# Sixteen small loads of each chunk's update, issued behind the seventh group's gradient loads

## The reference

```
step: g  = gradient of mean((mlp(params, k_t) - v_t)**2) by the parameters
      m  = eta_t * m - theta_t * g
      p  = (1 - alpha_t) * p + m
      out_t = mlp(p, q_t)           # after the new parameters
mlp(z) = silu(z @ (W0 + P0)) @ (W1 + P1)
```

## Time and profile before

| | |
|---|---|
| median of three runs | 12295.05 us |
| the profiled execution | 12288.19 us |
| its span | 12286.5 us |
| mean granted clock of TensorE | 0.881 of full |
| TensorE matmuls busy | 9695.2 us, 79 % |
| VectorE busy | 4669.4 us, 38 % |
| ScalarE busy | 1960.7 us, 16 % |
| GpSimd busy | 232.7 us, 2 % |
| DMA | 519.70 MB, mean 42 GB/s |

### The profile page before, as it was taken

One profiled execution on the slowest core, in us unless ns is written; L12 is line 12 of the kernel. 1 busy time (PEld: TensorE's weight loads), 2 busy tenths in 40 slices (PEclk: granted clock), 3 DMA queues, 4 the chain that ended last, 5 costly groups with the idle time before them and its releaser, 6 DMA issues. The chain is left out here.

```text
span 12286.5 us, 338221 instructions
## 1 busy us (share of the span) xinstructions
PE 9695.2 (79%) x135922; PEld 5708.6 (46%) x135922; DVE 4669.4 (38%) x11974; ACT 1960.7 (16%) x4398; POOL 232.7 (2%) x167
## 2 busy tenths in 40 slices
PE   5788883523598888888988988889888898896777
PEld 2455551212355555555555555555455555552222
DVE  3444443634723323233233233232332323235555
ACT  1222221211101101011011011110101101012334
POOL 0000000000100000000000000000000000000000
PEclk7999996555898998999999999989898798987888
DMA  2000000143601101011011011120211202020000
GB/s 55 7 7 8 7 8 25 42 123 61 138 17 53 51 18 52 23 47 53 17 53 53 17 53 57 42 81 17 82 45 54 81 17 82 26 72 14 13 10 10
DMA packets 894399, 519.70 MB, mean 42 GB/s; under 512 B 379950, under 2 KB 889462, under 8 KB 892534
## 3 DMA queue, kind: packets, MB, share of 16 engines
q1 hardware_dynamic: 880694, 502.37, 15.1%
q0 software_dynamic: 13312, 12.57, 0.6%
HBM read 323.24 MB, written 154.20 MB: 39 GB/s over the span
## 5 line engine op out<-in xcount | busy, mean ns | idle before, releaser
L2319 PE MATMUL bank<-mv,hdiag 128*32 128x144 f32 x63744 | 2038.0, 289 | 102.1 <-DVE hdiag L2480 102.1
L2319 PEld LDWEIGHTS bank<-mv,hdiag 128*32 128x32 f32 x63744 | 1950.0, 111 | 165.8 <-DVE hdiag L2480 151.2
L2359 PE MATMUL bank<-mvt,ydiag 128*32 128x512 f32 x15936 | 1830.3, 594 | 0.0
L2359 PEld LDWEIGHTS bank<-mvt,ydiag 128*32 128x32 f32 x15936 | 606.5, 109 | 807.8 <-issue 723.1
L2493 DVE TENSOR_TENSOR rep<-bank,wt 128x128 f32<-128x128 f32 x249 | 92.0, 369 | 1863.1 <-PE bank L2319 1863.1
L439 PE MATMUL att_bank<-att_ka,att_qn 128*124 128x496 f32 x1024 | 497.0, 598 | 133.6 <-DVE att_mx L616 67.0
L2423 DVE SCALAR_TENSOR_TENSOR mvt<-mvt,cu,bank 128x256 f32<-128x256 f32 x512 | 223.3, 478 | 791.3 <-PE bank L2254 791.3
L2216 ACT ACTIVATE work<-work 128x128 f32<-128x128 f32 x498 | 142.3, 309 | 2357.6 <-DVE work L2468 2357.6
L2203 ACT ACTIVATE mv<-bank 128x256 f32<-128x256 f32 x1024 | 325.1, 384 | 1091.1 <-PE bank L2267 1091.1
L459 PE MATMUL att_bank<-att_qa,att_ka 128*124 128x248 f32 x2048 | 464.7, 385 | 32.6 <-DVE att_qa L625 32.6
L2254 PE MATMUL bank<-hist,wy 32*128 32x256 f32 x2048 | 393.1, 544 | 90.4 <-DVE wy L2413 89.7
(11 more groups left out here) (402 smaller groups left out, 11450.9 us busy)
## 6 DMA issues: line engine op xcount, KB each, us to landing
hdiag<-between_slopes SPq DMA_DIRECT2D x368, 512.0 KB, 4.6
baset<-between_base SPq DMA_DIRECT2D x265, 128.0 KB, 2.0
between_base<-work SPq DMA_DIRECT2D x256, 128.0 KB
hist<-h SPq DMA_DIRECT2D x1992, 8.0 KB
hist<-y SPq DMA_DIRECT2D x1992, 2.0 KB
hist<-dl SPq DMA_DIRECT2D x1992, 8.0 KB
ct<-between_table SPq DMA_DIRECT2D x184, 128.0 KB, 3.8
between_slopes<-key_zero SPq DMA_DIRECT2D x8, 2048.0 KB
```

The source lines that it names most:

```text
L2319: mm = e.matmul(psP[32 * j:32 * j + 32, 0:MW], hdiag[:, hf, r, j, :], mv1[:, hf, r, j, :], start=(hf == 0 and r == 0), stop=(hf == 1 and r ...
L2359: mm = e.matmul(psH[32 * j:32 * j + 32, :], ydiag[:, n, j, :], mvt[:, 4 * n + j, :], start=(n == 0), stop=(n == 7))
```

## The change

The two loops that issue the sixteen loads become a function, `rows_of_table`. It is called in the loop over g, at g = 6, behind that group's gradient loads. The number of loads, their sources, targets and semaphores are as before.

```diff
+        def rows_of_table(e, c):
+            for i in range(8):
+
+                src = CT[bass.ds(c, 1), bass.ds(64 + c * CH, CH), :, :].rearrange("a s (m i) f -> s (a m) i f", m=2)[:, :, i, :]
+                e.dma_start(ccp[16 * i:16 * i + 16, 0:16 * CH].rearrange("p (m f) -> p m f", m=2), src).then_inc(cc_in.sem, 16)
+            for q in range(8):
+                row = CT[bass.ds(c, 1), bass.ds(64 + c * CH, 1), 0:1, :].rearrange("a s g f -> (a s g) f")
+                src = bass.AP(row.tensor, row.offset + (16 * q + 1), [[128, 16], [2049, CH - 1], [1, 1]])
+                e.dma_start(alt[16 * q:16 * q + 16, 1:CH].unsqueeze(2), src, allow_slow_non_contiguous=True).then_inc(al_in.sem, 16)
...
                     for xk in range(DX):
                         load_slopes(e, part, xk)
-                    for i in range(8):
...
-                        e.dma_start(ccp[16 * i:16 * i + 16, 0:16 * CH].rearrange("p (m f) -> p m f", m=2), src).then_inc(cc_in.sem, 16)
-                    at = 0
-                    for q in range(8):
...
-                        e.dma_start(alt[16 * q:16 * q + 16, 1:CH].unsqueeze(2), src, allow_slow_non_contiguous=True).then_inc(al_in.sem, 16)
                     for g in range(16):
                         e.wait_ge(T.sem, T.upd(c, f"bg{g}"))
                         settled(e, s_own)
...
                         if g % 2 and g // 2 + 2 < 8:
                             load_table(e, c, part, g // 2 + 2)
+                        if g == 6:
+                            rows_of_table(e, c)
                         if g % 2:
                             e.wait_ge(A.sem, A.upd(c, f"bs{g // 2}"))
```

More of the change, by code:

```diff
@@ L2133, in chunk @@
                         load_slopes(e, part, xk)
-                    for i in range(8):
-                        src = CT[bass.ds(c, 1), bass.ds(64 + c * CH, CH), :, :].rearrange("a s (m i) f -> s (a m) i f", m=2)[:, :, i, :]
-                        e.dma_start(ccp[16 * i:16 * i + 16, 0:16 * CH].rearrange("p (m f) -> p m f", m=2), src).then_inc(cc_in.sem, 16)
-                    at = 0
-                    for q in range(8):
-                        row = CT[bass.ds(c, 1), bass.ds(64 + c * CH, 1), 0:1, :].rearrange("a s g f -> (a s g) f")
-                        src = bass.AP(row.tensor, row.offset + (16 * q + 1), [[128, 16], [2049, CH - 1], [1, 1]])
-                        e.dma_start(alt[16 * q:16 * q + 16, 1:CH].unsqueeze(2), src, allow_slow_non_contiguous=True).then_inc(al_in.sem, 16)
                     for g in range(16):
```

## The result

The changed kernel takes 12356.81 us (median of four runs, 12350.34 to 12372.16), the kernel before 12291.96 us (four runs, 12281.11 to 12295.21). The ratio is 1.0056 with a 95 % interval of 1.0039 to 1.0074: it is slower by 0.56 %; the medians lie 65 us apart. The forecast was slower, 12397 us, in a range of 12335 to 12440. The direction and the range held; the size was too large by 40 us. The profiled execution's span is 12348.7 us, 62.2 us over the one before.

A forecast was written before the change was run, and what follows sets the result against it. TensorE sets the pace in the update, its waits for gradient loads being all the change can remove. Idle 32.2, clock 64.4 and 4.6, late chunks 1.1: 102.3 us slower, 12397 us on the runs' scale, range 12335 to 12440 us.

The forecast's parts named there:

- Nothing is gained in the early chunks' front: Chunks 0 to 8, front of the update: no load wait behind the sixteen, so moving them away saves 0.
- The late chunks' front wait goes: Chunks 9 to 15, group 1's second product: waits of 4.9 us in six, 3.02 in chunk 15 go; 32.4 us saved.
- Group 10's table rows come late: Chunks 0 to 8, group 10: TensorE idles 4.3 us in seven, 2.1 in chunk 1, none in chunk 3; 32.2 us.
- The middle wait of the late chunks: Chunks 9 to 15, group 8's second product: idle of 4.7 us in six, 5.3 in chunk 9; 33.5 us added.
- The clock falls with the idle: Chunks 0 to 8, behind group 10's 4.3 us idle: granted clock falls from 1.00 to near 0.5 to 0.7.
- What the fall costs: Chunks 0 to 8, group 10 to L2112: half-clock time adds 64.4 us in seven chunks, 4.6 in chunk 1.
- The rival in which the clock returns after 5 us: Behind the middle idle, full clock returns at once or after 5 us: +48, 12343 us; chance 0.13.
- The step put at nothing: Chunks 0 to 8, update up to group 7: moving the sixteen from the front saves 0, no clock change counted.
- The faster rival: Chunks 9 to 15: group 8's idle brings full clock back, -73 us; sum -40, 12255 us; chance 0.05.

The follow-up runs named there:

- Experiment 7: Changed kernel with the burst cut in two: eight cc loads behind group 6's gradient loads, eight alt behind group 10's; 12263.66 us, 0.9985 of the kernel before.
- experiment 2: Kernel before, with the sixteen loads moved behind group 6's gradient loads in chunks 9 to 15 alone; 12285.37 us, 1.0010 of the kernel before.
- Experiment 3: Changed kernel plus seven idle matmuls ahead of group 10's table-row wait in chunks 0 to 8; 12305.99 us, 1.0023 of the kernel before.
- experiment 8: One cc and one alt load behind each even group's gradient loads, idle matmuls in group 0's waits and late chunks' second-load waits; 12204.51 us, 0.9935 of kernel before.
- experiment 6: One cc and one alt load behind each even group's gradient loads, idle matmuls in group 0's two waits; 12239.70 us, 0.9963 of the kernel before.
- experiment 5: One cc and one alt load behind each even group's gradient loads, idle matmuls before second-load waits in chunks 9 to 15; 12201.85 us, 0.9938 of kernel before.
- experiment 4: Sixteen loads spread, one cc and one alt behind each even group's gradient loads in all chunks; 12251.11 us, 0.9974 of the kernel before.

## Why the prediction was right in direction and too large

- *Nothing is gained in the early chunks' front*: right as to the waits. Those for group 0's gradient load are 26.7 us in all after 27.1, those for its table rows 41.1 after 36.9, and there are no others for loads up to group 7.
- *The late chunks' front wait goes*: right. At group 1 no wait of 3 to 5 us is left; ahead of group 8 the seven updates have three waits over 1 us, of 1.5 us each.
- *Group 10's table rows come late*: right in place and mechanism. The sum said 4.3 us in seven chunks, 2.1 in one and none in one, 32.2 us; the trace has 3.4 to 4.2 us in all nine, 33.7 us, since in this execution all nine were at full clock by group 7. They are smaller than 4.3 because the burst was shorter: 10.85 us in chunk 2, not 11.24 (`alt` 3.95 after 5.13, `cc` 6.73 after 5.93). Experiment 7 shows the bound of 6.9 us from below.
- *The middle wait of the late chunks*: forecast 33.5 us, measured 26.6 (4.0, 3.9, 4.5, 4.0, 3.8, 3.9 and 2.5). The profile's late updates are longer by 15.6 us and not by 1.1, with more of their time at half clock, which the prediction had taken at 0 within bounds; but the whole edit there makes no difference that can be told (experiment 2).
- *The clock falls with the idle*: right, in nine chunks of nine, and experiments 3 and 7 show that it is the idle that does it.
- *What the fall costs*: forecast 69.0 us. From group 10's table product to L2112 the nine updates took 229.5 us after 166.2, 63.3 more. So the term was nearly right, though in another make-up: each fall cost less than forecast, 7.0 us and not 9.2 (19.7 us at half clock, not 23.6), and there were nine full falls and not seven and a half. Experiment 3's medians have some 41 us for the idle's clock, with 69 at the edge of what they leave. The rival in which the clock returns after 5 us, the rule of the Trainium skill's "TensorE: Matmul & The Clock Gate" (Part 1, on the HAM clock gate) taken alone, had 48 us in all. The trace disagrees with it: behind the idle TensorE worked 13.5 us or more at 0.50 in every one of the nine chunks. That its sum lies only 17 us below the measured 65 is luck.
- *The step put at nothing*: this is where most of the 40 us went. The early updates up to group 7 were 32.3 us shorter in the changed kernel's profile. The waits for loads are no shorter there; the time at half clock is, 191.7 us between the table products of groups 0 and 7 after 276.8, and at 0.39 us each these 85 us make 33. The forecast took the starts of the updates as they were in one execution, and that one stood at the slow end: the cut took 351.3 us there and 315.5 to 351.0, mean 332, in the profiles of the change and of the eight experiments. Whether a fall in one chunk's middle also shortens the next one's slow start stays open: the two kernels with the idle took 318.6 and 324.9 us, the others 328.8 or more, but experiment 8, without it, took 315.5, and experiment 6, with the same filling at the front, 339.6.

In the profile's own terms the early updates from group 7 on lost 89.6 us where the sum had 101.2 (7 us of the difference are groups 7 to 9 of chunks 1 and 3, which ran at half clock in part or whole before and at full clock after). With -32.3 up to group 7, +15.6 in the late chunks and -10.7 elsewhere that is 62.2. The mechanism was right; that the misses left the total inside the range is in part luck, since the late chunks' 14.5 us offset some of the others.

The faster rival needed full-clock groups behind the late chunks' middle idle. Two of seven had some (chunks 12 and 15); the other five stayed near 0.5. Its premise was read a little low: six of the seven late updates before, not five, had the full clock within 8 us of the front idle's end.

## What to carry to other kernels

When a burst of small transfers is moved in an issue queue, compare its length with the slack at the new place: the time from there to the next transfer's deadline, less its landing. 11 us at once cost some 65 to 70 us over nine chunks; the same loads as 6 and 5 us, or one pair at a time, cost nothing and brought 18 to 32 us. And an idle of a few us on TensorE has two prices, its own length and the clock behind it; filling it with matmuls that nobody needs separates the two, and where waits can't be avoided it can be worth shipping: it brought 44 us in experiment 5. But the filling has to last as long as the wait at full clock, once it has brought that clock (experiment 6). The kernel before already has such matmuls at the end of each step (`WARM = 3`, L2372).

## What the runs showed of the hardware that was not expected

- Work that waits less can run slower: in the late chunks of experiment 4 TensorE was busy 100.2 of 101.7 us at a granted 0.51, in experiment 5, with 30 more matmuls, 78.3 of 88.6 us at 0.94.
- At half clock a TensorE that hardly pauses can stay there for a whole update of 100 us (the same row of experiment 4), and one that works without a gap for more than half of one (54.00 of 54.00 us busy at 0.50 in chunk 0 of experiment 5). In group 0, with 128 x 128 matmuls in the waits (experiment 6), the full clock came within some 6 us. What keeps it low in the update's own mix of matmuls was not measured.
- SP's time for the same eight `alt` loads was 3.94 to 3.96 us in fifteen of the sixteen updates with the burst at group 6; at the front it was 4.3 to 5.4 us in fourteen of sixteen, and at group 10 (experiment 7) 4.0 to 5.5. The eight `cc` loads took 5.1 to 6.7 us against 5.2 to 6.6.
